# How the softmax shifts reach the queries: through TensorE and PSUM, or through 32x32 squares on VectorE and small DMAs

## The reference, cut to what matters

```python
q = (x @ Wq + bq).reshape(b, s, 16, 32).transpose(0, 2, 1, 3)
k = x @ Wk + bk                       # one key head and one value head of 32 channels
v = x @ Wv + bv
scores = jnp.einsum('bhsd,btd->bhst', q, k) / scale
attn = jax.nn.softmax(scores, axis=-1)
out = jnp.einsum('bhst,btd->bhsd', attn, v)
return out.transpose(0, 2, 1, 3).reshape(b, s, 512) @ Wo + bo
```

## Time and profile before

| | |
|---|---|
| median of three runs | 3122.11 us |
| the profiled execution, its time | 3151.85 us |
| its span, first to last instruction | 3150.1 us |
| attention's groups in the trace | about 817 to 2460 us |
| busy in the span: PE / DVE / ACT / POOL | 87% / 65% / 48% / 71% |

### The profile page before, as it was taken

One profiled execution on the slowest core, in us unless ns is written; L12 is line 12 of the kernel. 1 busy time (PEld: TensorE's weight loads), 2 busy tenths in 40 slices (PEclk: granted clock), 3 DMA queues, 4 the chain that ended last, 5 costly groups with the idle time before them and its releaser, 6 DMA issues. The chain is left out here.

```text
span 3150.1 us, 44567 instructions
## 1 busy us (share of the span) xinstructions
PE 2751.5 (87%) x15016; PEld 1648.4 (52%) x15016; DVE 2045.3 (65%) x3954; ACT 1523.3 (48%) x2871; POOL 2243.3 (71%) x1461
## 2 busy tenths in 40 slices
PE   7967777489899999999999999999999776888870
PEld 4644444266555555555555555555554474555540
DVE  7843222257788888788788887887874494333334
ACT  5622222153476666566566665765656451222220
POOL 2248888563399979799798897997989323778770
PEclk9979888689999999999999999999999767999995
DMA  5579999895388888799797887987877454999998
GB/s 209 212 208 247 236 237 240 182 287 193 84 183 180 170 179 177 153 194 181 165 184 159 188 166 157 194 173 174 175 149 165 139 211 136 221 234 241 234 183 325
DMA packets 221450, 608.27 MB, mean 193 GB/s; under 512 B 34476, under 2 KB 35500, under 8 KB 193320
## 3 DMA queue, kind: packets, MB, share of 16 engines
q0 software_dynamic: 91760, 376.49, 59.2%
q1 hardware_dynamic: 125240, 220.55, 21.3%
q10 hardware_dynamic: 4224, 8.39, 0.7%
HBM read 230.94 MB, written 155.24 MB: 123 GB/s over the span
## 5 line engine op out<-in xcount | busy, mean ns | idle before, releaser
L1924 DVE TENSOR_REDUCE attention_mx<-attention_pM 128x1 f32<-128x512 f32 x1984 | 1209.3, 682 | 185.1 <-PE attention_pM L1808 184.3
L1755 ACT ACTIVATE attention_prob<-attention_pS 128x512 f32<-128x512 f32 x2048 | 1032.7, 627 | 566.4 <-PE attention_pS L1787 561.7
L1692 POOL TENSOR_TENSOR attention_pair<-attention_prob 128x1024 f32<-128x1024 f32 x380 | 989.8, 2768 | 108.5 <-ACT attention_prob L1755 105.1
L1787 PE MATMUL attention_pS<-attention_qT,prep_kT 128*128 128x512 f32 x2048 | 841.3, 413 | 4.7 <-ACT attention_prob L1755 3.8
L1808 PE MATMUL attention_pM<-prep_kT,attention_qT 96*128 96x512 f32 x1984 | 787.8, 398 | 0.8
L1787 PEld LDWEIGHTS attention_pS<-attention_qT,prep_kT 128*128 128x128 f32 x2048 | 387.3, 189 | 313.0 <-issue 210.2
L768 POOL DMA_INDIRECT sum<-experts_res,c_table x256 | 403.5, 1576 | 124.3 <-issue 82.3
L1836 PE MATMUL attention_pO<-attention_prob,attention_v 128*32 128x512 f32 x4096 | 491.7, 598 | 0.0
L1808 PEld LDWEIGHTS attention_pM<-prep_kT,attention_qT 96*128 96x128 f32 x1984 | 377.9, 190 | 89.3 <-DVE attention_mx L1924 14.4
L752 POOL DMA_INDIRECT experts_rows<-xn_rows,c_table x256 | 250.1, 977 | 104.1 <-issue 74.9
L797 PE MATMUL experts_pT<-c_ident,experts_rows 128*128 128x128 f32 x1024 | 169.8, 307 | 117.1 <-issue 68.0
(11 more groups left out here) (184 smaller groups left out, 3195.3 us busy)
## 6 DMA issues: line engine op xcount, KB each, us to landing
prep_acc<-attention_pair POOLq DMA_DIRECT2D x96, 1024.0 KB, 8.1
attention_acc<-attention_pair POOLq DMA_DIRECT2D x90, 1024.0 KB, 7.7
attention_qT<-q_parts SPq DMA_DIRECT2D x96, 256.0 KB
xn_rows<-route_xn SPq DMA_DIRECT2D x16, 1152.0 KB, 6.6
experts_wup<-in_L_ffn_w_up_dram SPq DMA_DIRECT2D x64, 256.0 KB
q_parts<-prep_acc SPq DMA_DIRECT2D x64, 256.0 KB, 4.3
prep_acc<-prep_acc POOLq DMA_DIRECT2D x16, 1024.0 KB, 7.5
ahead_wup<-in_L_ffn_w_up_dram SPq DMA_DIRECT2D x64, 256.0 KB, 9.1
```

What stands on the lines that cost most here:

```text
L1692: pool.tensor_tensor(to[:, part], prob[2 * n % PROBS][:, part], prob[(2 * n + 1) % PROBS][:, part], ALU.add).then_inc(s_pair, 1)
L1755: act.activation(prob[t % PROBS][:, h * QT:(h + 1) * QT], pS[:, at, :], ACT.Exp).then_inc(s_ex, 1)
L1787: pe.matmul(pS[:, n % 3, :], kT[:, key:key + P], qT[g][:, h, :], start=True, stop=True).then_inc(s_sc, 1)
L1924: dve.tensor_reduce(mx[:, unit, part:part + 1], pM[:, r % RING, :], X, ALU.max).then_inc(s_mr, 1)
```

## The change

The shifts no longer pass through TensorE and PSUM. DVE writes them as two rows of sixteen numbers per query, `shift` [128, 2, 16], and turns this [128, 32] tile in 32x32 squares into `turned`. There 32 partitions belong to each block of 32 queries: sixteen for the shift of the 16 units (a unit is one head and one block of 128 queries), sixteen for the remainder. SP then moves them with 8 DMAs of [16, 32] float32 (2 KB) into single partitions, rows 96 and 97 of `qT[g]`. The score products read 98 rows instead of 128. Units are counted head first, so that such a row is contiguous in them. PE's first score product of a group waits for the 8 DMAs of that group, and DVE's next `make_shifts` waits for them too, since it overwrites `turned`.

```diff
-        shift = m.sb("shift", [P, HG, HG, DH])
+        shift = m.sb("shift", [P, 2, UNITS])
+        turned = m.sb("turned", [P, 2 * UNITS])
...
+                def place_shift(G):
+                    sp.wait_ge(s_turn, A + G + 1)
+                    for a in range(HG):
+                        for r in range(2):
+                            at, to = a * DH + r * UNITS, 3 * DH + r
+                            row = qT[G % GPC][to:to + 1, :, :].rearrange("p h (t n) -> p (h t) n", n=P).bitcast(F32)
+                            sp.dma_start(row[:, :, a * DH:(a + 1) * DH], turned[at:at + UNITS, :]
+                                         ).then_inc(s_row[G % 2], 16)
...
                     sp.dma_start(d_in[:, :], d_d[0, :, :].rearrange("h (j k) -> (h j) k", k=SPREAD)
                                  ).then_inc(s_di, 16)
+                    if G + 2 < GROUPS:
+                        place_shift(G + 2)
                     sp.wait_ge(s_rec, A + G + 1)
...
+                place_shift(0)
+                place_shift(1)
                 next_chunk(1)
...
-                        if t == 2 * COPY_PAIR + 1 and G + 1 < GROUPS:
-                            for h in (2, 3):
-                                copy_shift(G + 1, (G + 1) % GPC, h)
...
-                    if t == 0 and h < 2:
-                        pe.wait_ge(s_shd, A + G * 2 + h + 1)
-                    elif t == 0:
-                        pe.wait_ge(s_sha, A + G * 2 + h - 1)
+                    if t == 0 and h == 0:
+                        pe.wait_ge(s_row[G % 2], A + (G // 2 + 1) * 128)
                     key = batch * S + t * P
-                    pe.matmul(pS[:, n % 3, :], kT[:, key:key + P], qT[g][:, h, :], start=True, stop=True
-                              ).then_inc(s_sc, 1)
+                    pe.matmul(pS[:, n % 3, :], kT[0:SCORE_ROWS, key:key + P], qT[g][0:SCORE_ROWS, h, :], start=True,
+                              stop=True).then_inc(s_sc, 1)
...
-                    if p == COPY_PAIR and G + 1 < GROUPS:
-                        transposed_shifts(r, G + 1)
-                        r += 1
...
                     dve.wait_ge(s_mr, A + done)
+                    if G >= 1:
+                        dve.wait_ge(s_row[(G - 1) % 2], A + ((G - 1) // 2 + 1) * 128)
+                        dve.sem_inc(k["dve_on"], 1)
...
                     dve.wait_ge(s_mx, A + (G + 1) * 3)
-                    dve.tensor_reduce(shift[:, :, :, 1].rearrange("p t h -> p (t h)"), whole[:, :, :], X, ALU.add
-                                      ).then_inc(s_shift, 1)
...
+                        dve.tensor_reduce(shift[:, 1, :].bitcast(F32R), whole[:, :, :], X, ALU.add).then_inc(s_shift, 1)
+                    dve.wait_ge(s_shift, A + G + 1)
+                    dve.transpose(turned[:, :], shift[:, :, :].rearrange("p r u -> p (r u)")).then_inc(s_turn, 1)
...
-                dve.memset(shift[:, :, :, :], 0.0).then_inc(s_init, 1)
-                dve.wait_ge(s_init, 1)
                 make_shifts(0, 0)
-                for h in range(2):
-                    copy_shift(0, 0, h)
```

More of the change, by code:

```diff
@@ L1292, in first_maxima @@
                     unit, part = n // (S // 512), n % (S // 512)
-                    t, h = unit // HG, unit % HG
+                    h, t = unit // HG, unit % HG
                     if n == 0:
@@ L1538, in attention @@
         s_lon = m.sem("lon")
-        s_x = m.sem("x")
-        s_sha = m.sem("sha")
-        s_shd = m.sem("shd")
+        s_turn = m.sem("turn")
+        s_row = m.sems("row", 2)
         def o_raw(g):
@@ L1744, in _ @@
             def _(act):
-                begin(act, s_ex, s_sha)
+                begin(act, s_ex)
                 def exponential(G, t, h):
@@ L1768, in _ @@
                             exponential(G, t, h)
-                        if t == 2 * COPY_PAIR + 1 and G + 1 < GROUPS:
-                            for h in (2, 3):
-                                copy_shift(G + 1, (G + 1) % GPC, h)
             @block.tensor
             def _(pe):
-                begin(pe, s_sc, s_pv, s_lsum, s_mp, s_x)
+                begin(pe, s_sc, s_pv, s_lsum, s_mp)
                 def scores(G, t, h):
@@ L1820, in output @@
                     ins.then_inc(s_mp, 1)
[L1822 to L1828, removed]
                 def values(G, t):
```

37 lines of the change are left out of this document (8 added, 29 removed).

## The result

The changed kernel takes 3203.57 us (median of 5 runs, 3195.23 to 3207.12) against 3122.11 us before: a ratio of 1.0252, 95% interval 1.0241 to 1.0263. It is 81 us slower. The forecast was 3105 us and its range ended at 3138; both were wrong, in sign too.

What follows compares the result with a forecast made beforehand. PE was taken to bound the attention. Removing the transposes (-20.0 us) and a later start (+2.4) summed to -17.6 us, taking 3122.11 to 3104.5, stated as 3105 us; the 8-in-10 range was 3100 to 3138.

Steps and rivals of the forecast that it cites:

- PE bounds the attention, and removing the transposes gives 20.0 us: Attention: PE is always busy; dropping transposes saves 0.66 us in 22 plain groups and 0.61 in 9 output groups.
- The turned tile, the 98 rows: DVE's transpose with its wait takes 0.25 us (0.1 to 0.5); score products over 98 rows cost nothing more.
- A following issue costs 0.46 us in a quiet stretch and 1.26 under an accumulate.: SP's queue: rate per row DMA after the first, giving eight issues 3.6 us at least and 9.2 at most.
- Towards the end of an accumulate ... issues seem quick again; that I assume for 6, 7 and 8.: SP's last three row issues in the plain group shown: assumed quick, ending at 1472.2, 1472.6 and 1473.05.
- The step that failed: Plain groups: the eighth row DMA gets into the 0.6 us gap between POOL's accumulates, 3 us early, without PE waiting.
- the prediction's own sign of being wrong: Profile sign: 1 to 2 us waits before plain groups' first score product, most of all if eight issues exceed 7 us.
- The side that I took: Last row DMA before plain groups: taken to get in between the accumulates, not miss and be 1.6 us late; chance 0.46.
- The second rival: Plain groups: rows come after the second accumulate nearly everywhere, PE waits 35 to 55 us; 3140 to 3160, chance 0.23.
- The Trainium skill's rule of one packet in turn: DMA engines alternate queues by packet; read as one row DMA per accumulate, eight far too late; set aside.
- The start, +2.4: Start of attention: eight issues and landing behind Wo's load delay the first score product 2.4 us; bounds 1 and 7.
- Output groups wait for nothing: Output groups: two phases of 9.4 us leave over 20 us for the row DMAs, so no wait.
- The third rival: Attention: something else, POOL with 2.9 us slack, becomes late and holds PE; only part gained, 3112 to 3118, chance 0.07.

## Why the prediction was wrong, point by point

- **PE bounds the attention, and removing the transposes gives 20.0 us.** Right in place; 17.5 us measured in phase 6 of the changed kernel and 17.3 in the version with four DMAs and POOL's other order, whose plain group of 47.25 us is the 47.2 that was forecast.
- **The turned tile, the 98 rows.** Right: 0.212 us for the transpose; products over 98 and over 96 rows keep one rhythm.
- **"A following issue costs 0.46 us in a quiet stretch and 1.26 under an accumulate."** Too low on both sides. Those were averages from DMAs to 32 partitions each. The row DMAs' quick issues take 0.62 us ((4.99 us at the start) / 8), the slow ones 1.3 to 2.2 in the group shown.
- **"Towards the end of an accumulate ... issues seem quick again; that I assume for 6, 7 and 8."** Half right: in the group shown 6 and 7 took 0.59 us, and 8 then took 2.18.
- **The step that failed: the eight issues were to last 6.05 us and to end in the gap.** They take 7.1 us at the least and 7.9 in the median, 8.81 in the group shown; over 7 us was the prediction's own sign of being wrong. The gap itself stood where it was expected, 5.9 to 6.5 us behind the turned tile before and 6.2 to 6.6 now. Both mis-sizings count. The rates alone add about 1.2 us: in seven of the 22 groups with a wait the last issue was a quick one, and all eight still took 7.1 to 7.5 us. In the other 15 the last one was slow, and all eight took 7.7 to 10.6. Cutting the first accumulate (5.4 us for the eight) and halving the issues (3.6 us) both end the wait; cutting the second does too. So it is shown that the accumulate slows the issues, that their number counts, and that what is late waits for the second accumulate.
- **The side that I took.** The text itself put the issue's end at 1473.05 against a limit of "about 1473.1". A margin of 0.05 us on an assumed rate is no reason for 0.46 against 0.23. The limit was too late as well: it let the last pieces move 0.45 us after the issue's end, and in no group of the changed kernel was the last row packet through less than 0.81 us after it. "Where POOL is later the gap is later as well" held, and saved the two groups without a wait.
- **The second rival's price.** It was 35 to 55 us of waits, and 56.4 were measured, 22 waits of 1.8 to 4.4 us where I had 1.6 to 2.5. But it left out what PE does after a wait: 37.0 us of slower products in phase 0. With it the second rival would have been -17.5 - 1.3 + 3.6 + 56.4 + 37.0 = 78.2 us over the median of before, 3200.3 us; 3203.6 was measured. Without the clock it is 3163, and the kernel with PE kept busy took 3166.5.
- **The Trainium skill's rule of one packet in turn** ("DMA: Bandwidth & Descriptors", section on queues, rings and completion order). One row DMA let through per accumulate, as the prediction has it, does not follow from that rule: an accumulate is 128 packets of 8 KB in this trace, as many as a group has row packets, so that turns of one such packet each would let all rows through beside one accumulate. The trace stands between the two: 78 of 128 packets had passed by the end of the gap, 46 of them between 1715.5 and 1716.5, so the gap did let the waiting ones through at once, as I assumed; but of what came later 18 packets passed in 3.5 us of the second accumulate, and 32 around its end. Why those 32 stood still until 1720 while 18 had passed is not shown.
- **The start, +2.4.** 3.6 measured, from the issue of Wo's load: eight issues of 0.62 and not 0.46 make 1.3 us of difference.
- **Output groups wait for nothing.** Right, all of them.
- **The third rival, POOL's slack of 2.9 us.** I priced it at 0.07 since 0.66 us is taken from 2.9. But POOL's slack is no reserve on each group: inside it POOL also waits for its accumulates. With four DMAs in place of eight this cost 16.4 us, and another order on POOL took it away; with the rows in a spare tile it cost nothing, and why is open.

## What to carry to other kernels

Before small DMAs are put on a path that TensorE waits for, count their issues and not their bytes, at the rate that the trace shows beside the large transfer that will be running; if they must fit into a gap of half a microsecond, merge them until the margin is larger than the uncertainty of the rate. Price a wait of TensorE with what its clock loses after it; in this kernel that was two thirds of the wait again. And where one engine has a few per cent of slack over a period, look at what it waits for inside the period: work that is ready can be done in that wait, and in the kernel with four DMAs this order decided between no gain and 15 us.

## What the runs showed that I had not expected

- A wait of 1.8 to 4.4 us on PE was followed by products at half rate, 0.43 us apart: 7.31 us for a phase and not 5.79 mostly, behind 21 of 22 such waits. Why group 4, behind a wait of 2.2 us, escaped stays open. After two waits of 0.55 and 1.06 us in phase 4 the same 0.43 us rhythm appeared.
- At the start of attention, with no accumulate about, four DMAs of 32 packets issue in 2.77 us and eight of 16 in 4.99, which is 0.69 and 0.62 us each: the packets hardly count, the DMA does.
- SP's issues slow down while an accumulate of POOL's queue moves, from 0.6 to 1.4 us each and once in a while to 2.2, though SP itself does nothing else.
- An accumulate of POOL that lands late held POOL, ACT and PE one after the other: 4.39, 2.80 and, twice, 0.55 and 1.06 us in the group shown with four DMAs.
